# Graph network on one core: the product of slot matrix and fields in the message loop, made by GpSimd instead of VectorE

## The reference

```
B    = exp(-edge_weight)
msgs = B[:, None] * x[dst]
out  = segment_sum(msgs, src, 3125)
x    = layernorm(x + out)
```

## Time and profile before

| | |
|---|---|
| time, median of 3 runs | 3874.16 us (3871.46 to 3878.08) |
| the profiled execution's own time | 3872.01 us |
| its span | 3870.3 us |
| message loop within the span | about 205 to 735 us |
| busy over the span | PE 56%, weight loads 43%, DVE 69%, ACT 20%, POOL 52% |

### The profile page before, as it was taken

The page is one execution under the profiler, slowest core; times in us unless marked ns, Lnnn a source line. Parts: engine busy times, 40 slices in busy tenths (PEclk is TensorE's granted clock), DMA queues, the critical chain, the costliest instruction groups (busy, mean ns, idle before and its releaser), DMA issues. The chain is left out here.

```text
span 3870.3 us, 94308 instructions
## 1 busy us (share of the span) xinstructions
PE 2155.3 (56%) x24500; PEld 1651.6 (43%) x24556; DVE 2658.6 (69%) x5974; ACT 790.6 (20%) x1889; POOL 2002.5 (52%) x1981
## 2 busy tenths in 40 slices
PE   1435777555532555555555554356666566666497
PEld 0124666444432454445444443244444444444232
DVE  3898999877764677767777766467777777777511
ACT  1113444344420111111111111011111111111100
POOL 0024555322212777777777770377777777777000
PEclk9767888755555666666666665556666666666698
DMA  4035777666653666666666660255555555555587
GB/s 152 3 121 181 246 246 248 208 192 191 193 106 83 182 185 185 173 183 183 180 175 181 183 178 22 61 147 154 151 146 151 149 152 145 153 149 150 198 313 286
DMA packets 679637, 646.65 MB, mean 167 GB/s; under 512 B 129014, under 2 KB 513434, under 8 KB 678459
## 3 DMA queue, kind: packets, MB, share of 16 engines
q1 hardware_dynamic: 385403, 351.34, 30.4%
q0 software_dynamic: 77184, 154.07, 16.1%
q10 hardware_dynamic: 216796, 138.81, 11.6%
HBM read 433.74 MB, written 222.40 MB: 170 GB/s over the span
## 5 line engine op out<-in xcount | busy, mean ns | idle before, releaser
L1782 POOL DMA_INDIRECT rows<-nodes_xl,id_slot x832 | 821.8, 988 | 437.8 <-issue 246.1
L1782 POOL DMA_INDIRECT rows<-nodes_kv,id_slot x832 | 825.3, 992 | 320.5 <-issue 239.9
L1978 DVE SCALAR_TENSOR_TENSOR running_counts<-running_counts,same_block,counts_p 128x128 f32<-128x128 f32 x1144 | 394.6, 345 | 420.9 <-PE counts_p L2137 306.0
L2137 PE MATMUL counts_p<-hot_src,hot_blocks 128*128 128x128 bf16 x2288 | 293.5, 282 | 595.7 <-DVE running_counts L1978 594.1
L2137 PEld LDWEIGHTS counts_p<-hot_src,hot_blocks 128*128 128x128 bf16 x2288 | 218.5, 154 | 672.4 <-DVE running_counts L1978 608.9
L2181 PE MATMUL sums<-parts,hot 128*128 128x68 bf16 (+1 forms) x4992 | 325.3, 252 | 250.6 <-DVE parts L1962 250.6
L2181 PEld LDWEIGHTS sums<-parts,hot 128*128 128x128 bf16 x4992 | 311.8, 167 | 272.7 <-issue 272.7
L1062 POOL DMA_INDIRECT msg_by_src<-message,unit_slot x156 | 238.3, 1528 | 294.2 <-DVE message L923 263.9
L1219 PE MATMUL sums<-parts,hot 128*128 128x65 bf16 x3168 | 197.4, 244 | 179.4 <-DVE parts L1196 179.4
L1219 PEld LDWEIGHTS sums<-parts,hot 128*128 128x128 bf16 x3168 | 177.1, 132 | 200.4 <-issue 200.4
L1128 POOL DMA_DIRECT2D hot_src_by_cell<-hot x132 | 99.2, 752 | 282.9 <-DVE hot L1190 272.0
(11 more groups left out here) (475 smaller groups left out, 4290.1 us busy)
## 6 DMA issues: line engine op xcount, KB each, us to landing
hot_src<-hot_src_by_cell SPq DMA_DIRECT2D x1144, 64.0 KB
adjacency<-running_counts ACTq DMA_DIRECT2D x1144, 64.0 KB
hotT<-hotT_by_step SPq DMA_DIRECT2D x208, 256.0 KB
hot<-hot_by_step SPq DMA_DIRECT2D x208, 256.0 KB
blocks<-adjacency SPq DMA_DIRECT2D x40, 1280.0 KB
hot_src_by_cell<-hot POOLq DMA_DIRECT2D x132, 256.0 KB
rows<-msg_by_src SPq DMA_DIRECT2D x396, 68.0 KB
loc_all<-loc_by_cell SPq DMA_DIRECT2D x104, 256.0 KB
```

The lines of the kernel that those rows point to most:

```text
L1782: pool.indirect_dma_start(out=rows[:, j, t, :], out_offset=None, in_=table, in_offset=bass.IndirectOffsetOnAxis(ap=ids[:, j, t:t + 1], axis=0)
L1978: v.scalar_tensor_tensor(runs[:, r, q, :], before_it, same[:, bass.ds(J * BBODY + (count_from + q), 1)], counts_p[:, q - HALVES[q >= len(H ...
L2137: ins = nc.tensor.matmul(counts_p[:, q - HALVES[half][0], :], hot_b[:, r, :, t], hot_s[:, r, q, :, g], start=g == 0, stop=g == 1)
```

## The change

The product `moved` is taken out of VectorE's `order` and put, with the same operands, shape, buffers and semaphore, in a new `order` on GpSimd. GpSimd gets the same pipeline as the other engines: in the body of step k it makes the product for k+3 and then waits for `fill` of step k and scatters it. Its loop is now unrolled in the first three rounds and the last one, as on the others. It also waits on `in_order` itself, as VectorE did and still does for `unit_hot`.

```diff
@@ VectorE, order
                         v.tensor_tensor(unit_hot[:, s % 2, :, :], lane_u[:],
                                         u_h[:, bass.ds(J, 1), :].to_broadcast([P, P, WT6]), ALU.is_equal).then_inc(units_hot, 1)
-                        v.tensor_tensor(moved[:, s % 2, :, :, :],
-                                        slot_h[:, bass.ds(J, 1), :, :].rearrange("p a g r -> p (a g) r").unsqueeze(3)
-                                        .to_broadcast([P, WT6, US, FIELDS]),
-                                        rec_h[:, bass.ds(J, 1), :, :].rearrange("p a g f -> p (a g) f").unsqueeze(2)
-                                        .to_broadcast([P, WT6, US, FIELDS]), ALU.mult).then_inc(fields_moved, 1)
@@ GpSimd
-                    with pool.Fori(0, ROUNDS) as i:
-                        for s in range(N6):
-                            pool.wait_ge(filled, i * N6 + s + 1)
-                            pool.sem_inc(taken, 1)
-                            pool.indirect_dma_start(
...
+                    def order(i, s):
+                        J = i * N6 + s
+                        if not known(J, 2):
+                            pool.wait_ge(in_order, J - 1)
+                        nc.gpsimd.tensor_tensor(moved[:, s % 2, :, :, :],
...
+                                        .to_broadcast([P, WT6, US, FIELDS]), ALU.mult).then_inc(fields_moved, 1)
+
+                    def send(i, s):
+                        pool.wait_ge(filled, i * N6 + s + 1)
+                        pool.sem_inc(taken, 1)
+                        pool.indirect_dma_start(
...
+
+                    def step(i, s):
+                        for part_of, d in ((order, 3), (send, 0)):
+                            at = shifted(i, s, d)
+                            if inside(at[0]):
+                                part_of(*at)
+                    run(pool, step)
```

More of the change, by code:

```diff
@@ L1057, in _ @@
                     later["numbers"](pool)
-                    with pool.Fori(0, ROUNDS) as i:
-                        for s in range(N6):
-                            pool.wait_ge(filled, i * N6 + s + 1)
-                            pool.sem_inc(taken, 1)
-                            pool.indirect_dma_start(
-                                out=units_dram, out_offset=bass.IndirectOffsetOnAxis(ap=ids[:, s, :], axis=0),
-                                in_=rows[:, s, :, :].rearrange("p r w -> p (r w)"), in_offset=None, bounds_check=UNITS - 1,
-                                oob_is_err=False).then_inc(sent[s], 16)
+                    def order(i, s):
[3 more added lines that the diff above has]
+                        nc.gpsimd.tensor_tensor(moved[:, s % 2, :, :, :],
+                                        slot_h[:, bass.ds(J, 1), :, :].rearrange("p a g r -> p (a g) r").unsqueeze(3)
+                                        .to_broadcast([P, WT6, US, FIELDS]),
+                                        rec_h[:, bass.ds(J, 1), :, :].rearrange("p a g f -> p (a g) f").unsqueeze(2)
+                                        .to_broadcast([P, WT6, US, FIELDS]), ALU.mult).then_inc(fields_moved, 1)
[3 more added lines that the diff above has]
+                        pool.indirect_dma_start(
+                            out=units_dram, out_offset=bass.IndirectOffsetOnAxis(ap=ids[:, s, :], axis=0),
+                            in_=rows[:, s, :, :].rearrange("p r w -> p (r w)"), in_offset=None, bounds_check=UNITS - 1,
+                            oob_is_err=False).then_inc(sent[s], 16)
+                    def step(i, s):
[4 more added lines that the diff above has]
+                    run(pool, step)
                     for s in range(N6):
```

## The result

The changed kernel takes 3977.6 us (median of 4 runs, 3975.7 to 3984.2) against 3874.6 for the kernel before (4 runs): a ratio of 1.0264, 95% interval 1.0249 to 1.0278. The forecast was 3980. The number is right, the mechanism only in part, and that the two agree so closely is partly luck.

The account below looks back on a forecast made before the run. VectorE's instruction time was taken to bound the kernel before, at 3.00 us a step; afterwards a two-step GpSimd loop. Six terms sum to 7.50 us, 3.75 a step: 98 plus 10 us on 3872 gives 3980, range 3940 to 4015.

Parts of the forecast that it names:

- What bounded the kernel before: Message loop: VectorE's instruction time sets the step, busy 99.2 of 100 us, 3.00 us a step.
- The loop through GpSimd: Message loop: fill, scatter, product, three TensorE parts, fill close a two-step loop of 7.50 us, 3.75 a step.
- Terms 2 and 3: Parts of the GpSimd loop's sum: the scatter, 1.53 us, and the gap between two GpSimd instructions, 0.31 us.
- The lock: Rival: GpSimd's product and VectorE's instructions shut each other out, adding 0.34 us a step, 4028 us; chance 0.22.
- nothing changes: Claim that the code behind the message loop keeps its time, so the total grows by the loop's 108 us.
- 27 scatters in 100 us: Sign in the message loop's windows: 27 scatters in 100 us in place of 35.
- `sorted` 0.35 to 0.45 us behind each product: Sign on TensorE: sorted waits for GpSimd's products, about 0.4 us after each ends.
- products of 0.9 us: Sign on GpSimd: about 130 elementwise instructions of 0.9 to 1.3 us behind the scatters.
- about 65 to 75: Sign in the loop's windows: VectorE falls from 99 busy in 100 us to this, idling before numbers or pick_hot.
- over 90 would prove me wrong: Test in the message loop: the prediction is wrong if VectorE stays over 90% busy.
- longer `pick_hot` as the sign of the lock: With the lock, unit_hot, pick_hot or the product itself would be longer than their earlier rows.

Follow-up runs that it names:

- the gated kernel: Kernel after, product one step earlier, waiting for pick_hot's end, VectorE's numbers behind fill; 0.9932 and 0.9890 against the kernel before, loops 517.5 and 494.0 us.
- the control: Kernel before with only VectorE's numbers moved behind fill; ratio 1.0025 against the kernel before, 3899.7 us, message loop 523.6 us.
- product twice: Kernel after, with GpSimd making the same product a second time into a tile nobody reads; ratio 1.0360 against the kernel before, loop 734.1 us.
- both: Kernel after, but VectorE makes the product TensorE reads and GpSimd makes it too, unread; ratio 1.0309 against the kernel before, loop 703.5 us.
- one step earlier: Kernel after, with GpSimd's product at depth 4 in place of 3 and three buffers; ratio 1.0094 against the kernel before, loop 601.9 us.
- the one gated on `unit_hot`: The gated kernel, with the product waiting for the end of unit_hot in place of pick_hot; ratio 0.9911 against the kernel before, 3856.3 us.
- six fields on GpSimd: Kernel after, GpSimd's product without three weight fields after the first two steps, messages wrong; ratio 1.0058 against the kernel before, loop 577.6 us.
- the second trace: The gated kernel run again unchanged, in series 3; ratio 0.9890 against the kernel before, 3845.1 us, message loop 494.0 us.

## Why the prediction was right, and where it was not

**What bounded the kernel before: right.** VectorE at 99 leaves little else, and a product taken off it and held less brings a shorter loop (the gated kernel, 494.0 against the control's 523.6).

**The loop through GpSimd: there, but shorter than I made it.** The timeline after gives its terms: `fill` ends at 523.58, the scatter starts at 524.46 (0.88, as said); scatter 1.01 where I took the mean 1.53; gap 0.03 where I took 0.31 from another loop; product 0.92 for 1.10; to `sorted` 0.35 for 0.43; from there to the end of the narrowing, 526.77 to 528.84, 2.07, and with `pick` and `fill` unheld another 0.03 + 0.39 + 0.68, together 3.17 for 3.25. That is 6.36 us for two steps, 3.18 for one. By this loop alone the time would have risen by some 25 to 40 us, not 108; this is an estimate from 3.18 against 2.94 to 3.00 for a step. Terms 2 and 3 of the sum are the ones that were most mis-sized, by 0.8 us of the 1.1.

**The lock: the rival that I gave 0.22 carries most of the loss.** I had priced it at 0.34 us a step. It is 1.03: `pick_hot` 1.51 in place of 0.48 (500 to 600 us). I had counted only what one instruction may be late because of another. In fact the held one ends a fixed time behind the product, so VectorE loses the product's whole length, and a little more. And I had added it to the two-step loop: with `pick_hot` held, fill, scatter and product close a loop of one step, and that is what bounds the changed kernel, at 3.73 in every step. Shown by what is held when the product comes at another time (product twice, both, one step earlier) and by what isn't when it is gated.

**TensorE's clock as a rival.** It fell from 0.85 to 0.50, so slower matmuls could be thought to make the step longer. But no matmul stands between one `fill` and the next in the loop of 3.73, and with the product one step earlier, at a granted clock of 0.69 (500 to 600 us), the steps in which `pick_hot` is held take the same 3.73 to 3.74. No run changed the clock alone.

**The sum, as measured.** A step went from 2.94 to 3.73 us (420 to 620 us). On VectorE that is 0.52 off by the product that left, 1.03 on for the holding, 0.28 on for idle time ahead of `pick_hot` in the steps without a build. I had 3.00 and 3.75. Two errors met by luck: a data loop too long by 0.57 a step, and a hold that I had left to a rival and priced at a third. The rule of the Trainium skill that I cited as a rival's (SBUF — State Buffer, "Who interferes with whom") was right here against my estimate: an instruction of VectorE with two SBUF inputs (`unit_hot`, `moved`) is held by GpSimd's product, and so is the `tensor_scalar` form (`pick_hot`, `hotT`), while `fill`, with one SBUF input, isn't. The same section of the Trainium skill also says that whoever issues first keeps the port. By the recorded starts this can't be told: `pick_hot` starts 0.22 to 0.37 us before the product in the kernel after, up to 0.77 in the one gated on `unit_hot`, and is held all the same, while in the kernel with six fields on GpSimd it goes through from 0.28 before.

**The loop and the total.** I forecast 108 us for both. The loop lost 121, and 14 came back behind it, where I had written that nothing changes.

**The signs to look for.** 27 scatters in 100 us, `sorted` 0.35 to 0.45 us behind each product, products of 0.9 us: as written. VectorE "about 65 to 75" was wrong, 93. I had written that over 90 would prove me wrong, and for the mechanism it did: the records count an instruction that is held as busy. And I had named longer `pick_hot` as the sign of the lock.

## What to carry to other kernels

Before work moves from VectorE to GpSimd, list VectorE's instructions by what they read. Here those with two SBUF inputs and the `tensor_scalar` on bf16 could not run beside GpSimd's elementwise product, and those that read PSUM kept their times (`fill` 0.68, `numbers` 0.15 to 0.18). Unless the product is timed to meet the latter, VectorE gives it back (1.03 us for the 0.52 saved here), and the busy share hides it, as the time held counts as busy. An instruction whose mean grows on unchanged data is the sign.

And when a program-ordered engine gets a second job, write down the loop that its first job's wait closes. Here the extra buffer and the earlier product took 37 us off the loop (638.5 to 601.9), the gate and the order another 84 (to 517.5).

## What the hardware showed that I had not expected

- An instruction held by GpSimd's product ends a fixed time after it, in every trace in which it is held: `pick_hot` and `hotT` 0.28 to 0.30 us, `unit_hot` 0.42, `moved` 0.48. A start that is up to 0.77 us earlier than the product's by the records makes it end no sooner.
- A scatter isn't what holds: `unit_hot` keeps its 0.55 us beside scatters of 1.01 (528.19 and 528.23 after the change). `pick_hot` keeps its 0.48 beside one too, in the kernel before (560.19, in the scatter that began at 559.91). It is the scatter that grows: of the 79 scatters over 1.25 us in the kernel before (325 to 715 us), 73 end 0.19 to 0.21 us behind a `pick_hot` that ran within them. In the kernel after the long form is gone, but not in the gated kernels, although the product has left VectorE there as well: 36 of the 37 over 1.25 us in the second trace end 0.12 behind a `pick_hot`. No run moved `pick_hot` alone to test it.
- TensorE was granted 0.85 before, 0.50 after, and 0.95 in the gated kernel, with 73, 74 and 72 us busy in 100.
- GpSimd's product costs 0.92 us for 432 elements and 0.68 for 288 in bf16 with both inputs broadcast; beside a `pick_hot` that began ahead of it the latter took up to 0.89.
